# Graph sums left in PSUM banks, more buffers for the raw matrix, three blocks kept, and the bias moved into a matmul

## The reference

```python
def _L0_gnn_ref(x, evals, evecs, t):          # evecs is adj
    x_spec = jnp.einsum('nk,nc->kc', evecs, x)
    coefs = jnp.exp(-evals * t_eff)[:, None]
    return jnp.einsum('nk,kc->nc', evecs, coefs * x_spec)
def _L1_gnn_ref(inputs, adj, W, b):
    adj_hat = adj + jnp.eye(N, dtype=adj.dtype)
    deg = jnp.sum(adj_hat, axis=1, keepdims=True)
    out = adj_hat / deg @ (inputs @ W) + b
    return jnp.tanh(out)
x = _layernorm(x + _L0_gnn_ref(x, L0_gnn_evals, adj, L0_gnn_t), axis=-1)
x = _layernorm(x + _L1_gnn_ref(x, adj, L1_gnn_W, L1_gnn_b), axis=-1)
```

## Time and profile before

| | |
|---|---|
| time, median of 3 runs (lowest to highest) | 659.09 us (658.84 to 659.14) |
| the profiled execution: its time, its span | 658.01 us, 656.2 us |
| busy share of the span: PE, DVE, ACT, POOL | 90%, 80%, 60%, 56% |
| bytes moved, mean rate | 183.07 MB, 279 GB/s |
| mean granted TensorE clock | 0.974 |

### The profile page before, as it was taken

How to read it: one execution, slowest core, us unless ns; L and a number is a source line. 1 busy time by engine, 2 the same in 40 slices (tenths; PEclk the granted TensorE clock), 3 DMA queues, 4 the chain that set the end, 5 groups by cost and what they waited for, 6 DMA issues and landing times.

```text
span 656.2 us, 8010 instructions
## 1 busy us (share of the span) xinstructions
PE 590.7 (90%) x2444; PEld 449.2 (68%) x2444; DVE 524.6 (80%) x623; ACT 394.8 (60%) x856; POOL 364.3 (56%) x193
## 2 busy tenths in 40 slices
PE   3999999999984899999999999999997887879693
PEld 2888778877763565768887888888885554555451
DVE  3889888988887998888898877966668477795992
ACT  4999999999976446364656545544543443534332
POOL 0000000000234977978899997976679586977671
PEclk9999999999996999999999999999999798999897
DMA  8999999999999989999898987997769899999901
GB/s 277 388 387 386 387 386 387 387 387 387 386 306 304 292 237 288 279 305 269 223 268 247 261 237 184 255 221 183 213 153 269 174 308 310 262 231 358 320 24 33
DMA packets 149738, 183.07 MB, mean 279 GB/s; under 512 B 7108, under 2 KB 113860, under 8 KB 149704
## 3 DMA queue, kind: packets, MB, share of 16 engines
q1 hardware_dynamic: 93200, 125.87, 61.9%
q10 hardware_dynamic: 56504, 56.78, 32.8%
HBM read 180.52 MB, written 2.11 MB: 278 GB/s over the span
## 4 chain that ended last, share of the span: by engine, by line
PE 61%; POOL 14%; DVE 9%; ACT 6%; DMA 5%; issue 3%; ACTq 1%; SPq 0%; POOLq 0%; DVEq 0%
POOL lo L366 11%; PE ps L702 10%; PE ps L704 10%; PE ps L703 10%; PE ps L678 9%; PE ps L679 8%; PE ps L680 8%; DMA raw<-in_adj_dram 5%; DVE vt L533 4%; PE ps L698 4%; ACT hi L399 2%; ACT x_sb L454 2%; POOL rstd L358 2%; ACT hi L414 1%; DVE lo L540 1%
## 5 line engine op out<-in xcount | busy, mean ns | idle before, releaser
L366 POOL TENSOR_TENSOR lo<-vt,hi 128x1024 fp32r<-128x1024 f32 x133 | 330.8, 2513 | 92.8 <-ACT hi L414 92.1
L533 DVE STREAM_TRANSPOSE vt<-raw 128x1024 f32<-128x1024 f32 x200 | 240.3, 1224 | 78.5 <-PE ps L704 61.3
L414 ACT ACTIVATE hi<-vt 128x1024 fp32r<-128x1024 f32 x162 | 169.4, 1063 | 111.7 <-DVE vt L533 100.9
L516 DVE TENSOR_TENSOR lo<-raw,hi 128x1024 fp32r<-128x1024 f32 x124 | 153.3, 1239 | 21.5 <-ACT hi L399 20.9
L399 ACT ACTIVATE hi<-raw 128x512 fp32r<-128x512 f32 x256 | 158.2, 621 | 14.2 <-DMA raw<-in_adj_dram 5.9
L349 POOL TENSOR_TENSOR lo<-raw,hi 128x1024 fp32r<-128x1024 f32 x4 | 10.7, 2676 | 180.6 <-ACT hi L399 180.6
L678 PE MATMUL ps<-hi,xg_hi 128*128 128x512 f32 x256 | 102.9, 402 | 7.6 <-DVE lo L516 6.4
L702 PE MATMUL ps<-hi,s_hi 128*128 128x512 f32 x232 | 99.2, 427 | 8.2 <-issue 5.2
L702 PE MATMUL ps<-hi,p_hi 128*128 128x512 f32 x204 | 90.4, 443 | 14.9 <-POOL lo L366 14.9
L679 PE MATMUL ps<-lo,xg_hi 128*128 128x512 f32 x256 | 100.8, 394 | 0.0
L680 PE MATMUL ps<-hi,xg_lo 128*128 128x512 f32 x256 | 100.7, 393 | 0.0
(11 more groups left out here) (59 smaller groups left out, 523.5 us busy)
## 6 DMA issues: line engine op xcount, KB each, us to landing
raw<-in_adj_dram SPq DMA_DIRECT2D x64, 1024.0 KB, 14.3
raw<-in_adj_dram SPq DMA_DIRECT2D x104, 512.0 KB, 8.9
raw<-in_adj_dram ACTq DMA_DIRECT2D x104, 512.0 KB, 10.2
xn<-in_x_dram SPq DMA_DIRECT2D x8, 256.0 KB, 12.3
x_sb<-in_x_dram SPq DMA_DIRECT2D x8, 256.0 KB, 11.5
out_dram<-x_sb ACTq DMA_DIRECT2D x8, 256.0 KB, 5.2
rdeg<-out_dram SPq DMA_DIRECT2D x8, 2.0 KB, 9.3
w_sb<-in_L_gnn_W_dram ACTq DMA_DIRECT2D x1, 64.0 KB, 6.4
```

Of the source, the lines that this page charges most:

```text
L366: nc.gpsimd.tensor_tensor(lo[:, slot(p), :], vt[:, slot(p), :], hi[:, slot(p), :].bitcast(f32), ALU.subtract).then_inc(pool_lo_ready, 1)
L414: nc.scalar.activation(hi[:, slot(s), :], vt[:, slot(s), :], ACT.Copy).then_inc(hi_ready, 1)
L516: nc.vector.tensor_tensor(lo[:, q % RING1, :], raw[:, k, 2 * h:2 * h + 2, :].rearrange("p r n -> p (r n)"), hi[:, q % RING1, :].bitcast(f3 ...
L533: nc.vector.transpose(vt[:, slot(s), :].rearrange("p (m a i) -> p m a i", m=2, a=RB), load_buffer(st.load).rearrange("p (a m e i) -> p e m ...
```

## The change

Seven edits, made together.

1. Buffers: four (`BUFS = 4`) in place of three, and two more (`late_raw`) for stage 3, which lie over the hi and lo of the spectral coefficients and so come free with the last product of stage 2. `LOADS` takes the buffer that is freed first.
2. Kept blocks: units 1, 3 and 5 of the groups of the same number (their own diagonal blocks) stay in their buffer after the spectral product; their graph product is done in the stage 2 of the next group (visit 2, 4, 6), as soon as their p is known. Group 7's own unit is kept too and multiplied early in stage 3. Stage 3 has 16 loads of four steps each (`ORDER3`) in place of 20 loads, some of which served two steps; stage 2 has 134 steps in place of 128, stage 3 has 66 in place of 72.
3. Graph sums: each stays in one PSUM bank of its own (`BANK3`) to its end; only those of groups 0 and 1 are copied to `saves` and put back with a matmul by the identity. ACT's eight copies L476 fall to two, DVE's add L627 becomes an ACT copy.
4. b: added to p, on PE. Four matmuls with one row (`ones`, `b_bc[:1]`) go into p and four into the graph sum, in each of the eight endings. Since adj_hat's rows are divided by their own sum, p + b gives the same b. DVE's L632 falls away, and tanh takes 1/deg as its scale, in four pieces.
5. The norm's tasks stand at other positions: in stage 2 POOL at 4, ACT 7, PE 8, ACT 9, PE 10, ACT 11, DVE 12; in stage 3 ACT's copy 0, PE 1, tanh 3, add 4, statistics and means both 5, POOL 5, ACT 9.
6. In stage 3 DVE makes every tenth `lo` of the split steps; it made none.
7. `rsum` shares memory with other tiles; small constants are added.

```diff
-    BUFS = 3
+    BUFS = 4
+    BUFS3 = 6
...
+    ORDER3 = [(0, 0), (0, 1), (0, 2), (2, 1), (0, 3), (1, 1), (1, 2), (1, 3), (6, 3), (2, 2), (2, 3), (3, 2), (5, 3),
+              (3, 3), (4, 2), (4, 3)]
+    LOADS2 = [(g, u) for g in range(NG) for u in wides2(g)]
...
+    for n, (g, u) in enumerate(LOADS2):
+        units = (2 * u + 1, 2 * u) if 2 * u + 1 == g else (2 * u, 2 * u + 1)
+        for f in units:
+            WORK.append((n, f, True, f < g, g))
+            if n % NU == NU - 1 and g >= 2 and g % 2 == 0 and f == 2 * u:
+                WORK.append((n - NU, g - 1, False, True, g))
+    for i, (g, u) in enumerate(ORDER3):
+        if i == 4:
+            WORK.append((len(LOADS2) - 1, LAST, False, True, NG))
+        for f in (2 * u, 2 * u + 1):
+            WORK.append((len(LOADS2) + i, f, False, True, NG))
...
-        if not STEP[s].spectral:
-            return False
-        return SPLIT_COUNT[s] % 4 == 0 if STEP[s].group < 3 else s % 4 == 2
+        if STEP[s].visit == NG:
+            return SPLIT_COUNT[s] % 10 == 0
+        return SPLIT_COUNT[s] % 4 == 0 if STEP[s].visit < 3 else s % 4 == 2
...
+    BANK3 = {0: 7, 1: 2, 2: 3, 3: 4, 4: 5, 5: 6, 6: 7, 7: 2}
+    LATE3 = {0: 0, 1: 1}
...
                 for g in range(NG):
-                    if since2(p, g) == 5:
+                    if since2(p, g) == 4:
                         inverse_deviation(g % 2, g, mv2, ve2, pw2, rs2)
                 for row in range(NG):
-                    if since3(p, row) == 7:
+                    if since3(p, row) == 5:
                         inverse_deviation(row % 2, row, mv3, ve3, pw3, rs3)
...
+                if since == 0:
+                    act.wait_ge(mm_done, END3[g] + 1)
...
+                    nc.scalar.activation(stage[:, par, :], acc, ACT.Copy).then_inc(sum3, 1)
                 if since == 3:
-                    act.wait_ge(pre3, row + 1)
-                    nc.scalar.activation(acc_row(row), acc_row(row), ACT.Tanh).then_inc(tanh_ready, 1)
-                if since == 8:
...
+                    for r in range(R):
+                        last = nc.scalar.activation(acc[:, r * C:(r + 1) * C], acc[:, r * C:(r + 1) * C], ACT.Tanh,
+                                                    scale=rdeg[:, g, r:r + 1])
+                    last.then_inc(tanh_ready, 1)
+                if since == 9:
...
+                if first3 and carried:
...
+                    nc.tensor.matmul(acc3(g, NG), ident[:, :], saves[:, LATE3[g], :], start=True, stop=False)
...
-                if since == 9:
+                if since == 10:
                     pe.wait_ge(x1T_ready, g + 1)
                     for m in range(JB):
-                        nc.tensor.matmul(acc2(g)[:, m * C:(m + 1) * C], stage[:, 1, m * P:(m + 1) * P], w_sb[:, :],
-                                         start=True, stop=True)
...
+                        out_t = acc2(g)[:, m * C:(m + 1) * C]
+                        nc.tensor.matmul(out_t, stage[:, 1, m * P:(m + 1) * P], w_sb[:, :], start=True, stop=False)
+                        nc.tensor.matmul(out_t, ones[:, :], b_bc[:1, :], start=False, stop=True)
```

More of the change, by code:

```diff
@@ L24 @@
     graph: bool
-    row: int
+    visit: int
 def spectral_then_graph_conv(nc, x, adj, evals, t, W, b, out):
@@ L92, in spectral_then_graph_conv @@
[L92 to L94 removed]
+    ORDER3 = [(0, 0), (0, 1), (0, 2), (2, 1), (0, 3), (1, 1), (1, 2), (1, 3), (6, 3), (2, 2), (2, 3), (3, 2), (5, 3),
+              (3, 3), (4, 2), (4, 3)]
+    LOADS2 = [(g, u) for g in range(NG) for u in wides2(g)]
+    WORK = []
+    for n, (g, u) in enumerate(LOADS2):
[4 more added lines that the diff above has]
+                WORK.append((n - NU, g - 1, False, True, g))
@@ L95, in spectral_then_graph_conv @@
+    STEP = [Step(n, 2 * i + half == LAST_STEP[n], LOADS[n].group, f, half, spectral, graph, visit)
+            for i, (n, f, spectral, graph, visit) in enumerate(WORK) for half in range(2)]
     STEPS = len(STEP)
     BEFORE = [next((m for m in range(n - 1, -1, -1) if LOADS[m].buf == LOADS[n].buf), None) for n in range(NL)]
-    LAST_STEP = [max(s for s in range(STEPS) if STEP[s].load == n) for n in range(NL)]
     WHOLE_FROM = NK // 2
@@ L105, in whole @@
         st = STEP[s]
-        return st.half == 1 and st.unit >= WHOLE_FROM and (st.group < 3 or not st.spectral)
+        return st.half == 1 and st.unit >= WHOLE_FROM and (st.visit < 3 and st.spectral or st.visit == NG)
     SPLIT = [s for s in range(STEPS) if not whole(s)]
@@ L123, in spectral_then_graph_conv, with bank3 @@
     LATE_DVE = [q for q in range(PAIRS) if q % 4 != 1]
+    FIRST2 = [min(s for s in range(STEPS) if STEP[s].spectral and STEP[s].group == g) for g in range(NG)]
     END2 = [max(s for s in range(STEPS) if STEP[s].spectral and STEP[s].group == g) for g in range(NG)]
-    END3 = [max(s for s in range(STEPS) if STEP[s].row == r) for r in range(NG)]
-    FIRST = {}
-    FIRST_GRAPH = {}
+    END3 = [max(s for s in range(STEPS) if STEP[s].graph and STEP[s].group == g) for g in range(NG)]
+    ENDINGS = sorted(range(NG), key=END3.__getitem__)
+    KEPT1_END = max(s for s in range(STEPS) if STEP[s].graph and STEP[s].group == 1 and STEP[s].visit < NG)
+    BANK3 = {0: 7, 1: 2, 2: 3, 3: 4, 4: 5, 5: 6, 6: 7, 7: 2}
+    LATE3 = {0: 0, 1: 1}
+    def bank3(g, visit):
+        return LATE3[g] if visit == NG and g in LATE3 else BANK3[g]
+    FIRST3 = {}
     for s in range(STEPS):
[L131 to L135, removed]
+        if STEP[s].graph:
+            FIRST3.setdefault((STEP[s].group, bank3(STEP[s].group, STEP[s].visit)), s)
+    FIRST_OF_BANK = set(FIRST3.values())
+    POSITIONS = STEPS + LAG + 15
     def since2(p, g):
@@ L140, in since3 @@
     def since3(p, row):
-        return p - (END3[row] + LAG + 1)
+        return p - (END3[ENDINGS[row]] + LAG + 1)
     def landed(n):
@@ L492, in _ @@
                     ending2(g, since2(p, g))
+                if p == KEPT1_END + LAG + 2:
+                    act.wait_ge(mm_done, KEPT1_END + 1)
+                    act.wait_ge(xw_done, 2)
+                    nc.scalar.activation(saves[:, 1, :], acc3(1, 0), ACT.Copy).then_inc(saved, 1)
                 for row in range(NG):
                     ending3(row, since3(p, row))
+                if p == END2[LAST] + LAG + 1:
+                    for n in range(NL):
+                        if LOADS[n].buf >= BUFS and BEFORE[n] is None:
+                            wait_buffer(act, n)
+                            load_quarters(act, n, (2, 3))
             act.wait_ge(stored, 16 * NG)
@@ L708, in products @@
                 g = st.group
-                first = FIRST[g, st.row] == s
-                final = s == (END2[g] if st.spectral else END3[st.row])
+                first2 = st.spectral and s == FIRST2[g]
+                first3 = s in FIRST_OF_BANK
+                carried = st.visit == NG and g in LATE3
                 if whole(s):
@@ L716, in products @@
                     pe.wait_ge(s_ready, st.unit + 1)
-                if st.spectral and first and g >= 2:
+                if first2 and g >= 2:
                     pe.wait_ge(p_ready, g - 1)
```

138 lines of the change are left out of this document (71 added, 67 removed).

## The result

The changed kernel took 675.23 us (median of four runs, 667.65 to 680.77) against 658.97 for the kernel before. So the kernel is slower, which is clear of noise, but not surely by 2%. I had said 648 and 638 to 660. Its time also varies more than that of before, and goes with TensorE's mean granted clock: 667.65 us at 0.974, 673.04 at 0.966, 677.43 at 0.957, 680.77 at 0.952. The profiled execution is the first of these, so its rows show only part of what the median pays.

A forecast was written before the change was run, and what follows sets the result against it. PE was taken as the limit in stage 2. Stage 3's start at 514.0 (492.4 + 8.2 + 12.5 + 0.9), plus 118.2 for stage 3 and 13.1 of tail, gave a 645.3 span; forecast 648 us, range 638 to 660.

The forecast's parts named there:

- Part 3: b's eight matmuls on PE: 1.78 us an ending, +12.5 us ahead of stage 3, bounds 0 and 25.
- What bounds the kernel: Stage 2, groups 3 to 7: PE is busy throughout, so whatever it is given there adds to the time.
- Part 1: Buffers and order of stage 3: four loads fall away, all transfer waits (DVE's 12.6 us) are gone.
- the 5 us for what the count misses: Stage 3: allowance for waits beyond the counted 3.1 us, such as DVE's `lo` and a fallen clock; bounds 0 and 24.
- Part 2: Kept blocks: six split steps move from stage 3 to groups 2, 4 and 6; stage 2 grows by 8.2 us.
- Part 4: New places of the norm's tasks: `neg_mean` takes 0.17 us, both orders come out even, gain at most 0.3 a group.
- rival A: Stage 3 waits come from ACT's and POOL's task order, up to 24 us; time 659 to 667, chance 0.13.
- Stage 3: From first to last product: 110.1 us of PE work, 3.1 of waits and 5 more, 118.2 us long.
- The tail: From the last product to the span's end: 13.1 us, where it was 12.0.
- B: Half of rival A: some three us of waits at each double ending, or `neg_mean` at 1.2; 652 to 658, chance 0.2.
- C: The b matmuls cost little, or PE's growth in groups 2 to 7 is hidden; 634 us, chance 0.08.
- D: Stage 3 stays limited by transfers, if their rate falls under 230 GB/s; about 655 us, chance 0.04.

The follow-up runs named there:

- 64-row kernel: The changed kernel with every b matmul over 64 rows (a tile of 1/64) in place of one row: 660.68 us, ratio 1.002.
- kernel with b on DVE: The changed kernel with b added by DVE in stage 3 as before, no b matmuls, and tanh in one piece: 633.60 us, ratio 0.960.
- 128-row kernel: The changed kernel with every b matmul over 128 rows (a tile of 1/128) in place of one row: 646.44 us, ratio 0.980.

## Why the prediction was wrong, step by step

**The step that failed is Part 3**, the price of b on PE: "few rows save nothing. I take 1.78." Few rows save nothing, which is right, and they cost more, which I had no bound for: the matmuls with W and b of an ending took 5.36 where I had 3.53. The bound of 25 us covered wider records, not a longer distance between records of different row count. With 128 rows, where this distance is gone, the term is 1.78 as counted, and the whole kernel takes 646.44 against my 648.2. Of the 26.6 us between that and 673.04, 14.2 are the 80 changes at 0.18 us (shown by 64 rows against 128), and 12.4 come with one row and go with the granted clock. In the profiled execution, 6.1 us longer than that of the 64-row kernel (spans of 665.9 and 659.8), groups 3 and 5 of stage 2 are 6.3 longer (39.60 against 36.40, 45.00 against 41.90), the other groups less than 0.1. Of the longer executions only time and mean clock are known, so for the rest of the 12.4 the clock is argued and not seen. I shouldn't have read the four-row matmuls of the earlier trace rows as evidence. All eight have the same row count, so no change lies between them, and their 0.12 a record can't show one.

The page "TensorEngine Tiling (Array Packing)" of the Trainium skill, section "Key Properties", says that changing the tiling mode, not just the tile, drains TensorE. It lists row tilings of 128, 64 and 32 rows, and gives no time for the drain. The runs fit it, if a matmul over fewer rows than its neighbours counts as such a mode, which the page doesn't say: a weight load starts only with its own matmul behind a change, and a change costs 0.18 us, the same for 64 rows and for one. The prediction left that rule out, though it spoke against this change.

**What bounds the kernel** (PE in stage 2): right. What b on PE cost in stage 2 arrived in full in the time.

**Part 1, transfers gone**: right, 0.9 us in one place is left of 12.6. But four buffers would have done: without the two late ones the kernel with b on DVE takes 2.9 us less. What their issue costs ACT's queue stood nowhere in my sum, only within the 5 us for what the count misses.

**Part 2, +8.2 in stage 2**: right. In the 128-row kernel, which has my price for b, groups 3 to 7 of stage 2 take:

```profile
307.90:342.40 34.50, 34.50 (x167) 28.71 (x166) 29.94 (x31) 19.38 (x26) 33.41 (x16) 1.00 0.70 200
342.40:382.90 40.50, 40.21 (x191) 33.14 (x190) 33.27 (x35) 22.23 (x29) 38.07 (x18) 1.00 1.03 264
382.90:422.90 40.00, 40.00 (x192) 33.26 (x191) 28.23 (x32) 20.20 (x27) 31.22 (x15) 1.00 0.66 184
422.90:468.20 45.30, 45.30 (x215) 37.69 (x214) 34.32 (x34) 22.01 (x29) 34.69 (x17) 1.00 0.91 229
468.20:514.00 45.80, 45.80 (x216) 37.91 (x215) 28.21 (x32) 20.60 (x29) 34.06 (x17) 1.00 0.57 154
```

Before they took 32.7, 35.8, 38.2, 40.8 and 43.6: 1.8 more in groups 3, 5, 4.7 and 4.5 in groups 4 and 6, 2.2 in group 7, where I had 1.8, 4.5 and 1.8. Its stage 3 starts at 514.0, as I said.

**Part 4, the places of the tasks**: the size in stage 2 was about right (1.5 us between the starts of stage 3 with the old and the new places, where I had "come out even"), the reason half so: `neg_mean` took 0.17 in 11 of 16 cases and 0.87 to 1.92 in the rest, 0.57 on the mean. What I didn't price at all is their worth in stage 3, 17.5 us. The count that gave 118.2 went by the new places, so it held what they bring without naming it; the old places would have brought waits of the size of my rival A's.

**Stage 3**: right. 653.3 - 534.5 = 118.8 us in the changed kernel and 117.9 in the 128-row one (631.9 - 514.0), against 118.2; PE waits 6.5 us of the 8, 5.8 of it in the first 39 us. No queue falls behind at the double endings. The 36.5 us that I called waits in the stage 3 of before were not all waits: PE is idle for 26.5 there (36.6 - 30.7 and 115.0 - 94.4), and most of the rest goes with the clock of 0.91 and 0.96 in the same rows. The forecast of this stage didn't rest on it, but rival A's bound of 24 did. **The tail**: 12.6 against 13.1.

**The rivals.** A had the right side, with too low a time (659 to 667) and the wrong cause; B (652 to 658) was on neither count right: ACT's and POOL's order would have cost 20 us, but only with the tasks' old places. C had the error the other way round: its 634, b for nothing, is what the kernel takes without b, 632.3. None of mine had a price for b above 25 us in seven endings; 41 us in eight is what it costs. D's limit, the transfers, didn't show.

What stays open is what makes the clock fall with one-row matmuls in some endings and not in others. The runs show only where it fell and for how long, and that behind an ending it was rarer with 32 rows (one of four runs has a low mean clock, and the profiled one a single fall) and not seen with 64.

## What to carry to other kernels

Before a small matmul goes between others, compare its row count with theirs: over 128 rows with a scaled tile it cost no more here than its neighbours of the same width, each change of the row count cost 0.14 to 0.18 us, and standing the odd ones together left two changes of ten. A price from a row holds only for the neighbours that the row had. And a reordering of tasks has no worth of its own: here the same one brought 20 us in a kernel whose transfers were already early and 2.6 in one whose transfers weren't.

## What was unexpected of the hardware

- A change of row count between matmuls took 0.18 us (80 changes, 14.2 us), alike for 64 rows and for one; behind a change the weight load started together with its matmul, and otherwise 0.11 us ahead of it.
- Runs with ten changes an ending and one row had mean granted clocks of 0.947 to 0.974, the same instructions over 128 rows 0.981 to 0.984. Where it fell behind an ending of stage 2, PE had not stood idle, and eight small matmuls took 2.07 us instead of 1.15.
- Four quarter loads issued in a row by ACT kept its queue for 5.33 us, where two had taken 0.91 to 1.05 in the 60 us before, and the activation behind them started only then.
